# A 64-element pipeline on one core: key chunks in whole groups of four, the mask added in ScalarE's copy, one eps and one pow for two elements, and a PSUM bank moved from the scores to the expert layer

## The chip, the cores and the metric

The kernel runs on one core of a Trainium2 chip. A core has five engines with instruction streams of their own: TensorE (PE, matmuls), VectorE (DVE), ScalarE (ACT), GpSimd (POOL) and SyncE (SP, which issues the DMAs). They wait for each other by semaphores alone. The metric is the device time of one execution in microseconds (us); lower is better. 64 batch elements of 128 tokens by 128 channels pass through eight layers. The change touches the last two.

## What is computed

The reference, cut to those two layers (before each of them the input is normalised: mean subtracted, divided by the root of variance + 1e-5):

```python
# attention over 77 text keys, additive scores, one pair of gates per token
txt  = textual_features @ Ws;  feat = features @ W           # (64,77,128), (64,128,128)
h    = tanh(txt[:, None, :, :] + feat[:, :, None, :] + b)    # every token with every key
rho  = h @ w[:, 0]                                           # (64,128,77)
rho  = rho + (1 - q_masks)[:, None, :] * -1e30               # masked keys
att  = softmax(rho);  txt_h = att @ textual_features
x    = x + (tanh(txt_h @ Wcw.T + bcw) * features + tanh(txt_h @ Wcb.T + bcb))
# eight experts, each token to its best one, up to 1024 tokens for an expert over the whole batch
probs = softmax(xt @ wg);  mask = one_hot(argmax(probs), 8)
mask  = mask * (cumsum(mask, axis=0) - mask < 1024)
x     = x + gate * (mask * (xt @ W[e].T + b[e])) summed over e
```

## The kernel before, in words

`part_3` does these two layers, one batch element after the other. All steps of an element have names, `x3.*` for the attention, `r.*` for the score sums on TensorE, `t0`/`t1`/`t2` and `u0`/`u1` for the tanh of five key chunks, `f3.*` for the experts. Four tables (`PE_D`, `ACT_D`, `DVE_D`, `POOL_D`) set the order of the steps on each engine. One pass through a table is a *turn*; a step written `name@n` does, in turn p, its work for element p - n. So every engine works through the same list of steps 64 times, plus as many turns as the largest number behind an @, in which only some of the steps have an element. Each engine takes its list strictly in order: a step whose input is late holds up all that stands behind it on that engine. `Order.value(name, e)` is the semaphore value that says that this step of element e is done.

The way of element e before the change: VectorE takes mean and variance (`x3.stats`, `x3.aggr`, L2249, L2252); GpSimd adds eps (L2034), raises to the power -1/2 (L2037) and normalises (`x3.norm`, L2045); TensorE transposes (`x3.T`, L2160), ScalarE copies out of PSUM, TensorE projects text and features into bank `p_x` (`x3.proj`). For the 77 keys the sum text + feature is a 128-channel by 128-token tile for each key: VectorE makes keys 0 to 50 in three chunks of 17 (`x3.sum0` to `sum2`, tile `th`, L2268), GpSimd keys 51 to 76 in two chunks of 13 (`s.sum0`, `s.sum1`, tile `tl`, L2063). ScalarE takes the tanh in place (L2125, L2133). TensorE multiplies each key's tile with the vector w:

In `add`, key k goes to row a = k // 4 of group b = k % 4: the matmul writes the 32 partitions 32b to 32b+31 of the bank `p_rho`, by a weight tile of 32 columns of which one holds w (`tile_position=(0, 32 * b)`, so four keys with different b use different column quarters of the array). An f32 matmul is two instructions in the trace. The steps `r.rho0`, `r.rho1`, `r.rho2` take VectorE's chunks and `r.rhoP0`, `r.rhoP1` GpSimd's. Then ScalarE copies the bank out (`x3.rho`, tile `rs`, L2106), TensorE transposes it (`r.rhoT`, L2193) and adds the mask by a matmul of one row (L2194), VectorE takes the largest score (`x3.nmax`), ScalarE the exp, and so on to two gates per token, with which GpSimd ends the layer (`x3.y`, `x3.x`). There are two banks `p_rho`, for even and odd elements.

The expert layer normalises again (eps and pow of its own, L2034 and L2037), transposes (`f3.T`, L2211), routes (`f3.route`, L2214; `f3.nmax`, `f3.exp`, `f3.eq`, `f3.first`, `f3.pick`, L2303), counts places (`f3.place`, L2218, L2219), keeps those under the limit (`f3.keep`, `f3.kT`), multiplies by the experts (`f3.g`, L2228; `f3.xm`, L2311; `f3.y`, L2232 and L2234) and adds to x (`f3.out`, L2316). All its PSUM results but `p_g` lie in one bank `p_f`, so `f3.T` of element e waits for `f3.out` of e - 1. The mask is made in the part before, stored to `drop_rows` in memory and read back by SyncE as one row `drop`.

## Time and profile before

| what | value |
|---|---|
| median of 3 runs | 3001.69 us (2998.08 to 3005.58) |
| the profiled execution, its time | 3016.49 us |
| the profiled execution, its span | 3014.4 us |
| busy over the span: PE, DVE, ACT, POOL | 2681.1, 2458.3, 2251.8, 1419.1 us |
| the last part, from its first load issue to the end | 2193.6 to 3014.4 us |

The profile is one execution; its span runs from the first to the last instruction, and its time has 2.1 us more around the span. Times in the views are microseconds from the span's start. An engine's busy time is the union of its instructions; what is left is waiting. The last part fills the last 27% of the span.

### The profile page before, as it was taken

What the parts mean: (1) busy time and instruction counts of PE and PEld (TensorE: products, weight loads), DVE (VectorE), ACT (ScalarE), POOL (GpSimd) and SP (SyncE); (2) the same over time, 40 slices, a digit from 0 to 9 for tenths busy, and PEclk for the clock granted to TensorE, in tenths of its full rate; (3) what the DMA queues carried; (4) which work ended last, traced back from release to release, by engine and by line L of the source; (5) the groups of instructions that cost most, each with busy time, mean ns of one, the idle gap of its engine ahead of it and who ended that gap; (6) DMA issues with size and microseconds to landing.
All of it is one profiled execution on the core that took longest, in us unless ns stands there. A gap on an engine that the chain in (4) does not pass through costs nothing. (4 is left out here: it accounts for less than half of the span.)

```text
span 3014.4 us, 78117 instructions
## 1 busy us (share of the span) xinstructions
PE 2681.1 (89%) x28593; PEld 2003.6 (66%) x28593; DVE 2458.3 (82%) x6675; ACT 2251.8 (75%) x5270; POOL 1419.1 (47%) x2217
## 2 busy tenths in 40 slices
PE   6999999999999759979999998886669999999997
PEld 4666666666666549957767776332657777777776
DVE  5899989999999626559999997598668888888885
ACT  3899989999999614447777775298568888888884
POOL 1344434444444223335555552000068888888884
PEclk8999999999999869989999998899889999999998
DMA  1011111111111011101111110100210000000000
GB/s 50 27 35 52 56 38 35 35 35 35 35 34 31 20 55 49 48 21 34 34 34 34 34 33 16 27 0 0 77 38 16 16 16 18 16 16 16 17 15 8
DMA packets 177627, 91.14 MB, mean 30 GB/s; under 512 B 46339, under 2 KB 174021, under 8 KB 177251
## 3 DMA queue, kind: packets, MB, share of 16 engines
q1 hardware_dynamic: 171716, 76.85, 9.5%
q0 software_dynamic: 4096, 8.40, 0.9%
q8 instruction: 234, 3.83, 0.5%
q14 instruction: 141, 1.16, 0.1%
q10 hardware_dynamic: 1440, 0.90, 0.1%
HBM read 43.73 MB, written 42.36 MB: 29 GB/s over the span
## 5 line engine op out<-in xcount | busy, mean ns | idle before, releaser
L2268 DVE TENSOR_TENSOR th<-tf,p_x 128x2176 f32<-128x2176 f32 x192 | 463.2, 2413 | 8.0 <-ACT tf L2101 5.8
L2125 ACT ACTIVATE th<-th 128x2176 f32<-128x2176 f32 x192 | 386.4, 2012 | 0.0
L2063 POOL TENSOR_TENSOR tl<-tf 128x1664 f32<-128x1664 f32 x128 | 381.5, 2981 | 7.9 <-ACT tf L2101 7.9
L562 ACT ACTIVATE probf<-probf,colf 128x128 f32<-128x128 f32 x1024 | 313.2, 393 | 0.0
L2176 PE MATMUL p_rho<-th,late_w_row 128*32 128x128 f32 x6528 | 246.3, 276 | 0.0
L2176 PEld LDWEIGHTS p_rho<-th,late_w_row 128*32 128x32 f32 x6528 | 201.0, 110 | 15.2
L1675 PE MATMUL acc<-xnT_all,wT 128*128 128x512 f32 x384 | 181.8, 626 | 29.6 <-DVE tmax L1867 13.2
L2133 ACT ACTIVATE tl<-tl 128x1664 f32<-128x1664 f32 x128 | 202.8, 1585 | 3.6 <-POOL tl L2063 3.6
L452 POOL TENSOR_SCALAR col<-col 128x1 f32<-128x1 f32 x64 | 13.7, 214 | 395.5 <-DVE colc L887 344.5
L1094 POOL TENSOR_SCALAR col<-col 128x1 f32<-128x1 f32 x256 | 56.8, 222 | 271.5 <-DVE col L1383 191.6
L710 PE MATMUL fp<-ident,probf 128*128 128x128 f32 x1024 | 142.5, 284 | 24.6 <-ACT ygf L569 21.5
L566 ACT COPY probTf<-fp 128x1024 f32<-128x1024 f32 x128 | 129.5, 1012 | 46.3 <-PE fp L710 46.3
L1675 PEld LDWEIGHTS acc<-xnT_all,wT 128*128 128x128 f32 x384 | 73.5, 198 | 135.5 <-issue 83.5
L657 PE MATMUL xp<-ident,prob 128*77 128x128 f32 x1024 | 143.2, 284 | 20.0 <-DVE colc L903 18.8
L862 DVE TENSOR_TENSOR probf<-fs,causal 128x1024 f32<-128x1024 f32 x128 | 155.0, 1211 | 7.2 <-PE fs L698 7.2
L657 PEld LDWEIGHTS xp<-ident,prob 128*77 128x77 f32 x1024 | 115.0, 151 | 68.4 <-issue 65.8
L710 PEld LDWEIGHTS fp<-ident,probf 128*128 128x128 f32 x1024 | 114.7, 145 | 67.1 <-ACT ygf L569 48.5
L1097 POOL TENSOR_TENSOR col<-col,minus_half 128x1 f32<-128x1 f32 x256 | 146.3, 571 | 21.3
L698 PE MATMUL fs<-kblkf,qTf 32*128 32x512 f32 x512 | 149.5, 661 | 2.7 <-POOL kblkf L471 2.7
L865 DVE TENSOR_REDUCE colf<-probf 128x8 f32<-128x1024 f32 x128 | 149.1, 1203 | 0.0
L2027 POOL MEMSET cxT<- 128x51 f32 x9 | 0.8, 141 | 302.6 <-POOLq L1588 302.4
L1272 PE MATMUL p_gv<-w_conv,xqT 128*128 128x512 f32 x256 | 140.0, 629 | 0.0
(431 smaller groups left out, 8430.8 us busy)
## 6 DMA issues: line engine op xcount, KB each, us to landing
rows<-zeros SPq DMA_DIRECT2D x64, 256.0 KB, 2.4
cxT<-in_ctxT SPq DMA_DIRECT2D x128, 38.5 KB, 2.1
xb<-rows SPq DMA_DIRECT2D x67, 64.0 KB, 1.8
rows<-yb SPq DMA_DIRECT2D x67, 64.0 KB, 1.6
x<-in_x SPq DMA_DIRECT2D x64, 64.0 KB, 1.8
x_mid<-x SPq DMA_DIRECT2D x64, 64.0 KB, 1.5
z<-x_mid SPq DMA_DIRECT2D x64, 64.0 KB
x_next<-z SPq DMA_DIRECT2D x64, 64.0 KB, 1.5
```

The lines of the kernel that those rows point to most:

```text
L562: last = nc.scalar.activation(scores, scores, ACT.Exp, bias=colf[s][:, 16 + HALF * hf + h:17 + HALF * hf + h])
L657: last = nc.tensor.transpose(xp[0:KEYS, h // GROUP, (h % GROUP) * TOK:(h % GROUP + 1) * TOK], prob0[s][:, hf, h * KEYS:(h + 1) * KEYS], id ...
L698: last = nc.tensor.matmul(fs[:, b, :], qTf[s][g0:g0 + GROUP * HDIM, :], kblkf[s][g0:g0 + GROUP * HDIM, :, :], start=True, stop=True, tile_ ...
L710: last = nc.tensor.transpose(fp[:, h // GROUP, (h % GROUP) * TOK:(h % GROUP + 1) * TOK], probf[s][:, hf, h * TOK:(h + 1) * TOK], ident[:])
L862: nc.vector.tensor_tensor(scores, fs[:].rearrange("p b (h k) -> p (b h) k", h=GROUP), causal[:].unsqueeze(1).to_broadcast([128, HALF, TOK] ...
L865: nc.vector.tensor_reduce(colf[s][:, 16 + HALF * hf:16 + HALF * (hf + 1)], scores, X_AXIS, ALU.max, negate=True).then_inc(dve_done, DVE_L. ...
L1675: last = nc.tensor.matmul(acc[n][:, k, :], wT[:, m, k * CH:(k + 1) * CH], xnT_all[:, i * TTILE:(i + 1) * TTILE], start=True, stop=True)
L2063: nc.gpsimd.tensor_tensor(tl[i % NP][:, 0:shape[1], :], tf[s][:, POOLED[n]:POOLED[n + 1]].unsqueeze(2).to_broadcast(shape), tf[s][:, FEAT: ...
L2125: nc.scalar.activation(b, b, ACT.Tanh).then_inc(act_done, ACT_L.did(f"t{c}.tanh", e))
L2133: nc.scalar.activation(b, b, ACT.Tanh).then_inc(act_done, ACT_L.did(f"u{n}.tanh", e))
L2176: last = nc.tensor.matmul(p_rho[r][ROWS * b:ROWS * (b + 1), 0:TOK], w_row[:, ROWS - 1 - a:2 * ROWS - 1 - a], tanh[:, k, :], start=(a == 0) ...
L2268: nc.vector.tensor_tensor(th[i % NT][:, 0:shape[1], :], tf[s][:, CHUNK[n]:CHUNK[n + 1]].unsqueeze(2).to_broadcast(shape), p_x[r][:, AT:AT ...
```

## The change

Five things are changed in the last part. (1) VectorE's chunks are 16, 16 and 20 keys, GpSimd's 12 and 13. (2) The mask is no longer added by a matmul: `x3.rho` becomes an activation with the function Identity and a column `drop[:, e]` as its bias; that column tile is made once at the start by a transpose on TensorE and a copy on ScalarE, and the store to `drop_rows`, its load and their waits are gone. `r.rhoT` becomes one transpose instruction. (3) GpSimd's steps `x3.eps`, `x3.rstd`, `f3.eps`, `f3.rstd` become `n.eps` and `n.rstd`, each of which works on two columns, for `x3` of element j and `f3` of element j - 4; the means and variances lie in a new ring `mv`. (4) There is one bank `p_rho`; `r.rho0` of an element waits for `x3.rho` of the one before. The bank that comes free is `p_y` and takes `f3.place`, `f3.kT` and `f3.y`; `f3.T` waits only for `f3.pick` of the element before, and `f3.place` for its `f3.out`. Rings `xf`, `xfT`, `colf` have three buffers in place of two. (5) The four tables are new, and the largest number behind an @ is 9 in place of 6.

```diff
-    def __init__(self, text, count):
+    def __init__(self, text, count, longer=()):
+        longer = dict(longer)
         words = [(name, int(n or 0)) for name, _, n in (word.partition("@") for word in text.split())]
-        turns = range(count + max([n for _, n in words], default=0))
-        self.order = [(name, p - n) for p in turns for name, n in words if 0 <= p - n < count]
+        counts = {name: count + longer.get(name.partition(".")[0], 0) for name, _ in words}
+        turns = range(max([counts[name] + n for name, n in words], default=0))
+        self.order = [(name, p - n) for p in turns for name, n in words if 0 <= p - n < counts[name]]
...
 PE_D = """
-    f3.y@6 r.rho0@2 f3.T@5 r.rhoT@3 f3.route@5 r.rhoP0@2 r.rho1@2 f3.place@5 x3.T r.rhoP1@2 f3.kT@5 x3.proj f3.g@5
-    p.PT@3 r.rho2@2 p.gate@3
+    r.rho0@4 r.rhoT@5 r.rhoP0@4 f3.y@9 r.rho1@4 f3.T@7 f3.place@8 r.rhoP1@4 r.rho2@4 x3.T@2 p.PT@5 f3.kT@8
+    f3.route@7 x3.proj@2 p.gate@5 f3.g@8
 """
 ACT_D = """
-    x3.xT x3.exp@3 f3.kT@5 t0.tanh@1 x3.PT@3 x3.proj t1.tanh@1 u1.tanh@1 x3.gate@3 x3.rho@2 f3.xT@4 u0.tanh f3.exp@4
-    t2.tanh@1
+    t1.tanh@2 x3.gate@4 f3.exp@6 x3.proj@1 t2.tanh@2 x3.exp@3 u1.tanh@2 t0.tanh@1 f3.xT@5 u0.tanh@1 x3.xT x3.rho@2
+    x3.PT@3 f3.kT@6
 """
 DVE_D = """
-    f3.eq@6 f3.first@6 f3.pick@6 f3.stats@5 x3.nmax@4 f3.aggr@5 f3.keep@6 x3.sum1@2 x3.rden@4 f3.xm@6 x3.sum2@2
-    x3.gb@4 f3.out@6 x3.sum0@1 x3.stats f3.nmax@5 x3.aggr f3.rden@5
+    x3.sum0@3 f3.pick@8 x3.aggr@2 f3.out@9 f3.stats@6 x3.rden@5 f3.aggr@6 x3.sum1@3 f3.keep@8 x3.sum2@3 f3.nmax@7
+    x3.gb@5 f3.xm@8 f3.rden@7 x3.nmax@4 f3.eq@7 f3.first@7 x3.stats@1
 """
 POOL_D = """
-    f3.taken@5 x3.eps x3.rstd x3.norm f3.eps@4 s.sum1@1 f3.rstd@4 f3.norm@4 s.sum0 x3.y@3 x3.x@3
-"""
-
+    f3.norm@7 s.sum0@3 n.eps@2 n.rstd@2 x3.norm@2 f3.taken@7 s.sum1@3 x3.y@5 x3.x@5
+"""
+
+F3_LAG = 4
...
+    POOL_L = Order(POOL_D, BATCH, dict(n=F3_LAG))
+    NR, NX, NT, NF = 9, 4, 4, 3
     ROWS = 32
-    CHUNK = (0, 17, 34, 51)
+    CHUNK = (0, 16, 32, 52)
     CHUNKS = len(CHUNK) - 1
-    POOLED = (51, 64, KEYS)
+    POOLED = (52, 64, KEYS)
     POOLS = len(POOLED) - 1
     NP = 4
-    DTILE, PTILE = CHUNK[1], POOLED[1] - POOLED[0]
+    NV = F3_LAG + 2
+    DTILE = max(b - a for a, b in zip(CHUNK, CHUNK[1:]))
+    PTILE = max(b - a for a, b in zip(POOLED, POOLED[1:]))
...
-        drop = sb("drop3", [1, BATCH * WIDE], BF16)
+        before_bf, ones_bf, ident_bf, w_txt, w_feat, w_row, w_gate, b_gate, w_route, w_exp, pick_row, b_bf, drop_tile = (shared["late"][k] for k in (
+            "before_bf", "ones_bf", "ident_bf", "w_txt", "w_feat", "w_row", "w_gate", "b_gate", "w_route", "w_exp", "pick_row", "b_bf", "drop_tile"))
+        drop = sb("drop3", [128, BATCH])
...
-        p_rho = [ctx.enter_context(nc.psum_tensor(f"p_rho{s}", [128, BANK], F32)) for s in range(2)]
         p_x = [ctx.enter_context(nc.psum_tensor(f"p_x{s}", [128, BANK], F32)) for s in range(2)]
-        p_rT, p_f = (ctx.enter_context(nc.psum_tensor(n, [128, BANK], F32)) for n in ("p_rT", "p_f"))
+        p_rho, p_rT, p_f, p_y = (ctx.enter_context(nc.psum_tensor(n, [128, BANK], F32)) for n in ("p_rho", "p_rT", "p_f", "p_y"))
...
-            def rstd(p, e, c):
-                pool.wait_ge(dve_done, DVE_L.value(f"{p}.aggr", e))
-                nc.gpsimd.tensor_scalar(c[:, 8:9], c[:, 7:8], LN_EPS, None, ALU.add).then_inc(pool_done, POOL_L.did(f"{p}.eps", e))
-                yield
-                own(f"{p}.eps", e)
-                nc.gpsimd.tensor_tensor(c[:, 9:10], c[:, 8:9], minus_half[:, 0:1], ALU.pow).then_inc(pool_done, POOL_L.did(f"{p}.rstd", e))
+            def pair(j):
+                v = mv[j % NV]
+                here = slice(0 if j < BATCH else 1, 2 if j >= F3_LAG else 1)
+                n = here.stop - here.start
+                if j < BATCH:
+                    pool.wait_ge(dve_done, DVE_L.value("x3.aggr", j))
+                if j >= F3_LAG:
+                    pool.wait_ge(dve_done, DVE_L.value("f3.aggr", j - F3_LAG))
+                nc.gpsimd.tensor_scalar(v[:, 4 + here.start:4 + here.stop], v[:, 0:4].rearrange("p (n m) -> p m n", m=2)[:, 1, here], LN_EPS, None, ALU.add).then_inc(pool_done, POOL_L.did("n.eps", j))
+                yield
+                own("n.eps", j)
+                nc.gpsimd.tensor_tensor(v[:, 6 + here.start:6 + here.stop], v[:, 4 + here.start:4 + here.stop], minus_half[:, 0:n], ALU.pow).then_inc(pool_done, POOL_L.did("n.rstd", j))
                 yield
 
             def x3(e):
                 s, q = e % NX, e % NR
-                c = col[s]
-                yield from rstd("x3", e, c)
-                own("x3.rstd", e)
-                nc.gpsimd.tensor_scalar(xn[s][:], x[q][:], c[:, 6:7], c[:, 9:10], ALU.subtract, ALU.mult).then_inc(pool_done, POOL_L.did("x3.norm", e))
+                c, v = col[s], mv[e % NV]
+                own("n.rstd", e)
+                nc.gpsimd.tensor_scalar(xn[s][:], x[q][:], v[:, 0:1], v[:, 6:7], ALU.subtract, ALU.mult).then_inc(pool_done, POOL_L.did("x3.norm", e))
...
-                nc.scalar.copy(rs[r][:], p_rho[r][:, 0:TOK]).then_inc(act_done, ACT_L.did("x3.rho", e))
+                nc.scalar.activation(rs[r][:], p_rho[:, 0:TOK], ACT.Identity, bias=drop[:, e:e + 1]).then_inc(act_done, ACT_L.did("x3.rho", e))
...
+            act.wait_ge(drop_pe, 1)
+            nc.scalar.copy(drop[:], p_rT[:, 0:BATCH // 2].bitcast(BF16)).then_inc(drop_in, 1)
+            act.wait_ge(drop_in, 1)
...
-                    if c == 0 and e >= 2:
-                        pe.wait_ge(act_done, ACT_L.value("x3.rho", e - 2))
+                    if c == 0 and e >= 1:
+                        pe.wait_ge(act_done, ACT_L.value("x3.rho", e - 1))
...
-                nc.tensor.matmul(p_rT[:, 0:WIDE], rs[r][:], ident[:], start=True, stop=False)
-                nc.tensor.matmul(p_rT[:, 0:WIDE], ones_bf[0:1, :], drop[:, e * WIDE:(e + 1) * WIDE], start=False, stop=True).then_inc(pe_done, PE_L.did("r.rhoT", e))
+                nc.tensor.transpose(p_rT[:, 0:WIDE], rs[r][:], ident[:]).then_inc(pe_done, PE_L.did("r.rhoT", e))
...
                 if e >= 1:
-                    pe.wait_ge(dve_done, DVE_L.value("f3.out", e - 1))
-                nc.tensor.transpose(p_f[:, 0:TOK], xf[r][:], ident[:]).then_inc(pe_done, PE_L.did("f3.T", e))
+                    pe.wait_ge(dve_done, DVE_L.value("f3.pick", e - 1))
+                nc.tensor.transpose(p_f[:, 0:TOK], xf[s][:], ident[:]).then_inc(pe_done, PE_L.did("f3.T", e))
                 yield
                 pe.wait_ge(act_done, ACT_L.value("f3.xT", e))
-                nc.tensor.matmul(p_f[:, 128:128 + MOE3], xfT[r][:], w_route[:], start=True, stop=True).then_inc(pe_done, PE_L.did("f3.route", e))
+                nc.tensor.matmul(p_f[:, 128:128 + MOE3], xfT[s][:], w_route[:], start=True, stop=True).then_inc(pe_done, PE_L.did("f3.route", e))
                 yield
                 pe.wait_ge(pool_done, POOL_L.value("f3.taken", e))
                 pe.wait_ge(dve_done, DVE_L.value("f3.pick", e))
-                nc.tensor.matmul(p_f[:, 144:144 + MOE3], before_bf[:], pick[e % 4][:], start=True, stop=False)
-                nc.tensor.matmul(p_f[:, 144:144 + MOE3], ones_bf[:], taken[e % 4][:], start=False, stop=True).then_inc(pe_done, PE_L.did("f3.place", e))
+                if e >= 1:
+                    pe.wait_ge(dve_done, DVE_L.value("f3.out", e - 1))
+                nc.tensor.matmul(p_y[:, 144:144 + MOE3], before_bf[:], pick[e % 4][:], start=True, stop=False)
...
+            nc.tensor.transpose(p_rT[:, 0:BATCH // 2].bitcast(BF16), drop_tile[:], ident_bf[0:BATCH, 0:BATCH]).then_inc(drop_pe, 1)
+            pe.wait_ge(drop_in, 1)
```

How the tables put the instructions on the engines is best seen in the order itself. TensorE before, most of one turn in the steady state, from `f3.y` to the next `x3.T` and the second GpSimd chunk (the name of the tile written, the tiles read, its shape; xN is N keys or experts):

```order
L2232 MATMUL p_f<-late_b_bf,keptT 128x128
L2234 MATMUL p_f<-w_pair,xm 128x128 x8
L2176 MATMUL p_rho<-th,late_w_row 32x128 x17
L2211 MATMUL p_f<-ident,xf 128x128
L2193 MATMUL p_rT<-ident,rs 128x128
L2194 MATMUL p_rT<-drop,late_ones_bf 128x128
L2214 MATMUL p_f<-late_w_route,xfT 128x8
L2176 MATMUL p_rho<-tl,late_w_row 32x128 x13
L2176 MATMUL p_rho<-th,late_w_row 32x128 x17
L2218 MATMUL p_f<-pick,late_before_bf 128x8
L2219 MATMUL p_f<-taken,late_ones_bf 128x8
L2160 MATMUL p_x<-ident,xn 128x128
```

TensorE with the change, from the first score block of a turn to `x3.T`:

```order
L2186 MATMUL p_rho<-th,late_w_row 32x128 x16
L2203 MATMUL p_rT<-ident,rs 128x128
L2186 MATMUL p_rho<-tl,late_w_row 32x128 x12
L2243 MATMUL p_y<-late_b_bf,keptT 128x128
L2245 MATMUL p_y<-w_pair,xm 128x128 x8
L2186 MATMUL p_rho<-th,late_w_row 32x128 x16
L2220 MATMUL p_f<-ident,xf 128x128
L2229 MATMUL p_y<-pick,late_before_bf 128x8
L2230 MATMUL p_y<-taken,late_ones_bf 128x8
L2186 MATMUL p_rho<-tl,late_w_row 32x128 x13
L2186 MATMUL p_rho<-th,late_w_row 32x128 x20
L2170 MATMUL p_x<-ident,xn 128x128
```

The row of the mask (L2194) is gone. The blocks of a turn were 17, 13 + 17, 13 (behind `x3.T`) and 17 keys (later in the turn); now they are 16, 12, 16 and 13 + 20, where a + says that two chunks stand back to back. `f3.y` stood ahead of all of them and now stands between the second and the third, and `x3.T` follows the last of them at once.

VectorE before, from `f3.out` (L2316) on, where sum0 (L2268), the two moments of x3 (L2249, L2252) and the routing follow:

```order
L2316 SCALAR_TENSOR_TENSOR x<-p_f,colf,x 128x128
L2268 TENSOR_TENSOR th<-tf,p_x 128x2176
L2249 BN_STATS col<-x 128x6
L2290 TENSOR_REDUCE colf<-p_f 128x1
L2252 BN_AGGR col<-col 128x2
L2293 RECIPROCAL colf<-colf 128x1
```

VectorE with the change, the same neighbourhood:

```order
L2261 BN_STATS col<-x 128x6
L2282 TENSOR_TENSOR th<-tf,p_x 128x2048
L2319 TENSOR_SCALAR pick<-p_f,colf 128x8
L2264 BN_AGGR mv<-col 128x2
L2332 SCALAR_TENSOR_TENSOR x<-p_y,colf,x 128x128
L2261 BN_STATS colf<-x 128x6
L2289 RECIPROCAL col<-col 128x1
L2264 BN_AGGR mv<-colf 128x2
L2282 TENSOR_TENSOR th<-tf,p_x 128x2048
```

Before, the long sum stood between `f3.out`, which waits for `f3.y`, and the moments of x3; now the moments' first step stands ahead of sum0, `x3.aggr` (the first L2264) ahead of `f3.out`, and only two short rows between `f3.out` and `f3.aggr` (the second L2264).

GpSimd before, one turn from `x3.eps` on:

```order
L2034 TENSOR_SCALAR col<-col 128x1
L2037 TENSOR_TENSOR col<-col,minus_half 128x1
L2045 TENSOR_SCALAR xn<-x,col 128x128
L2034 TENSOR_SCALAR colf<-colf 128x1
L2063 TENSOR_TENSOR tl<-tf 128x1664
L2037 TENSOR_TENSOR colf<-colf,minus_half 128x1
L2074 TENSOR_SCALAR xf<-x,colf 128x128
L2063 TENSOR_TENSOR tl<-tf 128x1664
```

GpSimd with the change, from `n.eps` on:

```order
L2041 TENSOR_SCALAR mv<-mv 128x2
L2044 TENSOR_TENSOR mv<-mv,minus_half 128x2
L2051 TENSOR_SCALAR xn<-x,mv 128x128
L2089 TENSOR_TENSOR taken<-taken,pick 128x8
L2069 TENSOR_TENSOR tl<-tf 128x1664
L2055 TENSOR_SCALAR xn<-xn,col 128x128
L2058 TENSOR_TENSOR x<-xn,x 128x128
L2079 TENSOR_SCALAR xf<-x,mv 128x128
```

An eps and a pow of one column each are gone, and the remaining two work on two columns; the normalisation of the expert layer now stands most of a turn behind them.

## Rows read from the trace of the kernel before

**Rows 1.** Windows: us; busy of PE, PEld, DVE, ACT, POOL; PEclk; DMA share, GB/s.

```profile
2300.00:2900.00 600.00, 556.60 (x9845) 462.91 (x9843) 517.93 (x887) 528.14 (x793) 500.43 (x546) 1.00 0.06 17
2960.00:3014.40 54.40, 38.83 (x461) 31.90 (x453) 21.99 (x60) 17.34 (x40) 13.62 (x26) 0.81 0.03 8
```

**Rows 2.** Waits, 2300 to 2900 us: TensorE's; total us, times, longest.

```profile
PE p_x L2160 <- POOL xn L2045: 28.5, 49, 0.6
PE p_f L2218 <- DVE pick L2303: 14.0, 47, 0.3
```

**Rows 3.** Timeline of one turn: start, us, engine, line; in brackets the idle before.

```profile
2600.28 0.33 PE L2160 MATMUL p_x<-ident,xn 128*128 128x128 f32 x1 [0.58 <-POOL xn L2045]
2600.54 1.06 PE L2176 MATMUL p_rho<-tl,late_w_row 128*32 128x128 f32 x26
...
2603.51 1.28 PE L2176 MATMUL p_rho<-th,late_w_row 128*32 128x128 f32 x34
...
2605.19 2.05 PE L2234 MATMUL p_f<-w_pair,xm 128*128 128x128 f32 x16
...
2607.36 0.35 DVE L2316 SCALAR_TENSOR_TENSOR x<-p_f,colf,x 128x128 f32<-128x128 f32 x1 [0.32 <-PE p_f L2234]
...
2608.87 0.23 PE L2194 MATMUL p_rT<-drop,late_ones_bf 1*128 1x128 bf16 x1
...
2609.07 0.39 PE L2214 MATMUL p_f<-late_w_route,xfT 128*128 128x8 f32 x2
...
2610.56 0.23 POOL L2034 TENSOR_SCALAR col<-col 128x1 f32<-128x1 f32 x1 [1.58 <-DVE col L2252]
...
2611.54 0.81 POOL L2045 TENSOR_SCALAR xn<-x,col 128x128 f32<-128x128 f32 x1
...
2612.40 0.33 PE L2160 MATMUL p_x<-ident,xn 128*128 128x128 f32 x1 [0.58 <-POOL xn L2045]
```

**Rows 4.** Windows of L2176 alone, from the start of one block of 17 keys.

```profile
2615.63:2615.76 0.13, 0.13 (x4) 0.13 (x8) 1.00 0.00 0
2615.63:2616.50 0.87, 0.87 (x32) 0.87 (x33) 1.00 0.00 0
2615.63:2616.60 0.97, 0.97 (x33) 0.97 (x34) 1.00 0.00 0
2615.63:2616.70 1.07, 1.07 (x34) 1.01 (x34) 1.00 0.00 0
```

**Rows 5.** Groups by line and shape, whole span: busy us, mean ns, idle before.

```profile
L2268 DVE TENSOR_TENSOR th<-tf,p_x 128x2176 f32<-128x2176 f32 x192 | 463.2, 2413 | 8.0 <-ACT tf L2101 5.8 <-PE p_rho L2176 2.0
...
L2063 POOL TENSOR_TENSOR tl<-tf 128x1664 f32<-128x1664 f32 x128 | 381.5, 2981 | 7.9 <-ACT tf L2101 7.9
...
L455 POOL TENSOR_TENSOR colf<-colf,minus_half 128x2 f32<-128x2 f32 x64 | 46.4, 725 | 5.3
...
L2037 POOL TENSOR_TENSOR col<-col,minus_half 128x1 f32<-128x1 f32 x64 | 36.4, 568 | 5.3
...
L1143 ACT ACTIVATE qT<-p_gv,b_xa 128x128 f32<-128x128 f32 x64 | 23.5, 367 | 12.8 <-PE p_gv L1245 12.6
...
L2106 ACT COPY rs<-p_rho 128x128 f32<-128x128 f32 x64 | 15.3, 239 | 0.0
```

**Rows 6.** Timeline: the first sum, then `f3.out` and the last turn.

```profile
2202.09 2.42 DVE L2268 TENSOR_TENSOR th<-tf,p_x 128x2176 f32<-128x2176 f32 x1 [5.19 <-ACT tf L2101]
...
2255.66 0.35 DVE L2316 SCALAR_TENSOR_TENSOR x<-p_f,colf,x 128x128 f32<-128x128 f32 x1 [0.68 <-PE p_f L2234]
...
2970.10 0.35 DVE L2316 SCALAR_TENSOR_TENSOR x<-p_f,colf,x 128x128 f32<-128x128 f32 x1
...
3001.45 0.35 DVE L2316 SCALAR_TENSOR_TENSOR x<-p_f,colf,x 128x128 f32<-128x128 f32 x1 [4.17 <-PE p_f L2234]
...
3004.46 0.17 PE L2218 MATMUL p_f<-pick,late_before_bf 128*128 128x8 bf16 x1 [1.47 <-DVE pick L2303]
...
3012.05 0.35 DVE L2316 SCALAR_TENSOR_TENSOR x<-p_f,colf,x 128x128 f32<-128x128 f32 x1 [4.13 <-PE p_f L2234]
```

86 lines of the change are left out of this document (42 added, 44 removed).

## The prediction, made before the changed kernel ran

> **What bounds the kernel now.** I read the windows first, to see which stage the change touches and how full its engines are; then the waits of that stage, which name what an engine stood idle for; then the timeline of one turn, to follow the loop that sets its length. The reader is to see three things. In the steady state the granted clock is 1.00 (the 2.4 GHz level) and in 600 us PE is busy 556.6, ACT 528.1, DVE 517.9 and POOL 500.4 us [rows 1]: nobody is full. One turn lasts 2612.40 - 2600.28 = 12.12 us, from one `x3.T` to the next [rows 3]. So 600 us hold 49.5 turns, and one turn costs PE 11.24, ACT 10.67, DVE 10.46 and POOL 10.11 us of work. PE's missing 0.88 us are nearly two waits: for `x3.norm` (28.5 us in 49 turns, 0.58 each) and for `f3.pick` (0.3 each) [rows 2].
>
> The loop behind the first wait is in the timeline. PE goes from `x3.T` (2600.28) without a stop through its list to the end of `f3.y` (2605.19 + 2.05 = 2607.24); DVE has waited for this and makes `f3.out` at 2607.36; then its list has the long sum0 ahead of `x3.stats` and `x3.aggr`, so GpSimd starts eps only at 2610.56, after 1.58 us of idleness, and ends the normalisation at 2612.35; PE's next `x3.T` is at 2612.40 [rows 3]. That is 6.96 us of PE, 3.3 of DVE, 1.8 of POOL: the whole 12.12 us. PE alone would need 11.24. So two things are to be asked: what the new tables make of this loop, and what work each engine has per turn.
>
> **The change part by part.** *Key chunks.* Within a block of 17 keys (34 instructions) the starts come in bursts of four: 4 in the first 0.13 us, 32 by 0.87, and then the last two alone, one between 0.87 and 0.97 and one by 1.07 [rows 4]. So a burst step is about 0.11 us, four keys with their two instructions each take two steps, and the 17th key takes two more steps for itself. A check: the block of 13 keys has 6 full steps and 2 single ones, that is 7 intervals of 0.11 and one matmul of some 0.28, together 1.05; the row has 1.06 [rows 3]. The 17: 9 intervals, 1.00 + 0.28 = 1.28; the row has 1.28 [rows 3]. Counted in rounds of four keys, the blocks of a turn before are 17, 13 + 17, 13, 17: 5 + 8 + 4 + 5 = 22 rounds (in the double block the second chunk begins with the group that the first has just not used). Now they are 16, 12, 16 and 13 + 20. The last begins its second chunk with the same group that ended the first, so it takes 3 + 1 + 5 = 9, and the sum is 4 + 3 + 4 + 9 = 20. Two rounds less are 4 x 0.11 = 0.44 us of PE per turn. If there were nothing to the rounds and only the number of keys counted, it would be 0, since there are 77 before and after; both ends are kept.
>
> *The mask.* The matmul of one row began at 2608.87 and the next instruction at 2609.07: 0.20 us of PE per turn [rows 3]. The one-pass transpose may give 0.06 more; I take nothing. On ScalarE the copy of 239 ns becomes an Identity with a column as bias. The nearest row is L1143, the same function and shape out of PSUM with such a bias: 367 ns [rows 5], so ACT pays 0.13 us. The Trainium skill ("ScalarE: Activation LUTs", What ACT_TABLE_LOAD costs) puts a pointer operand at about 93 ns; by that the price would be 0.09, and 2 us less over 64 turns. The transpose and copy that make `drop` stand at the start of the part, where PE has nothing until the first x has come, and cost nothing; without that cover it would be under 1 us, once. The DMAs taken away from SP had no one waiting for them.
>
> *One key more for VectorE.* 2413 ns for 17 keys are 0.14 us a key [rows 5]: DVE +0.14. GpSimd's key is 2981 / 13 = 0.23 us less. ScalarE's tanh covers 77 keys as before.
>
> *eps and pow.* One eps of 0.23 [rows 3] and one pow of 0.57 go; the pow of two columns takes 0.725 (L455) in place of 0.568 [rows 5]. POOL: -0.23 - 0.57 + 0.16 - 0.23 = -0.87. It is no bound, so this is worth nothing by its size; what counts is where it stands.
>
> *The sums per turn.* PE 11.24 - 0.44 - 0.20 = 10.60; ACT 10.67 + 0.13 = 10.80; DVE 10.46 + 0.14 = 10.60; POOL 10.11 - 0.87 = 9.24. An engine's busy time is a little more than its need, since instructions whose inputs are there overlap, as `x3.T` and the block behind it by 0.07 [rows 3], so 10.6 is possible and 10.8 is what ACT's sum says. If the new tables let the engines run, a turn takes 10.8.
>
> *Do they?* The old loop is cut: `x3.stats` now stands ahead of sum0 and `x3.aggr` before `f3.out`, so no long sum lies between `f3.y` and the eps. What joins them now is the common eps, which also waits for `f3.aggr` of the element four behind. From the end of `f3.y`: 0.12 to `f3.out`, 0.3 for it, then `f3.stats`, the reciprocal and `f3.aggr`: 0.7 by estimate from the 0.23 of another short row, 1.05 if each took the 0.35 of `f3.out`; then 2.0 on POOL (2610.56 to 2612.35, and 0.16 for the wider pow) [rows 3, 5]. That is 3.1 to 3.4 us. In PE's list `r.rho1` (1.05), three short steps (0.2 each, as the mask's) and the double block (17 intervals of 0.11 and 0.28, 2.15) stand between `f3.y` and `x3.T`: 3.8, less 0.1 to 0.2 where they overlap. It arrives in time with 0.2 to 0.5 us to spare. I laid the other handovers out in this way, each engine's list from such durations; most have 0.1 to 0.5 us to spare at 10.6, `x3.rho` 2 us (below). With so many near the edge a few tenths of waiting would be no surprise: that is the range's upper part.
>
> *Filling and emptying.* Now: the first sum at 2202.09, `f3.out` of element 0 at 2255.66, of element 59 at 2970.10 (59 turns, 12.11 each), the end at 3014.4 [rows 1, 6]. With the change the largest lag is 9 in place of 6. Filling: 8.5 us to the first sum as now, then six turns up to the first `f3.out` instead of five. The five took (2255.7 - 2202.1) / 5 = 10.7 each, 1.4 less than a full one; six of 10.8 - 1.3 = 9.5 are 57, with the 2.5 us by which `f3.out` stands behind sum0 in DVE's list 68 in all, against 62. Then 57 full turns to `f3.out` of element 57: 57 x 10.8 = 616. Emptying: six turns, against four in 42 us. The two first still have most of the attention in them: 9.5 and 8. The last four hold the expert layer alone. Such a turn took 3012.05 - 3001.45 = 10.6, of which 2.7 lie between the end of `f3.out` and `f3.place`: transposing, routing and choosing [rows 6]. These no longer stand behind `f3.out`, since `f3.T` waits only for `f3.pick`: 8.0 each, 32. With the 2.3 us after the last `f3.out`: 52, against 44.
>
> **The sum.** The last part takes 68 + 616 + 52 = 736 us, against 3014.4 - 2193.6 = 820.8 now: -85. The profiled execution (span 3014.4, time 3016.5) becomes a span of 2930 and a time of 2932; it was 14.8 us above the median of the runs, so the median becomes 3001.7 - 85 = **2917 us** (-2.8%).
>
> **The rivals.**
> *Handovers bind* (0.20). The lists are right in their work, but one of the tight handovers costs each turn 0.3 to 0.9 us; the turn is 11.1 to 11.7. For it: three engines within 0.2 us of each other leave no room, and now they lose 1.3 to 1.6 us a turn. Against it: each loop that I followed closes below 10.6. At 11.4: 57 x 0.6 = +34, 2951 us.
> *Rounds don't count* (0.07). If a key costs the same in any block, PE keeps 11.04 and sets the turn: +14, 2931. The single last bursts speak against it [rows 4]. The Trainium skill ("TensorE: Matmul & The Clock Gate", Part 3: Packing small matmuls) has a group of column tiles take the time of one matmul plus some 4 ns each; the trace agrees with its bursts, and by that page an unfilled group costs a full one, as in my sum.
> *The single bank* (0.04), the one on the other side. With two banks PE could write one while ACT read the other; now `r.rho0` stops PE until ACT has read `p_rho`. Behind the last block PE has `x3.T`, four steps (2603.51 - 2600.28, less the block of 1.06: 2.2 with `x3.T`) and two pairs of 0.39: 2.9 us [rows 3]. The copy has to be done in that time, and in ACT's list a tanh of 12 keys and the copy after `x3.T` stand ahead of it; from `x3.T` on it needs 0.33 + 0.24 + 0.37 [rows 3, 5] and handovers, about 1.0. It decides when ACT runs 2 us behind; the gain is gone when each turn waits 1.5 us more than that. At 2 us of waiting a turn is 12.8: 68 + 730 + 52 = 850, 3031 us. The Trainium skill speaks for this rival ("PSUM — Partial Sum Buffer", Summary: rules for kernel authors: for reading PSUM while a matmul runs, target a different bank).
> *No change* (0.02): half of the two before, a turn of 12.2.
> *More than forecast* (0.07): the engines overlap better, a turn of 10.5, or the clock stays up in the emptying: 17 + 10 less, 2890.
>
> **How the numbers follow.** The forecast has 0.60, with a turn of 10.6 to 11.0, so 2905 to 2929 us. The range for 8 in 10 takes in the rounds, most of the handovers (up to 11.4 with a longer emptying) and part of the better case: 2896 to 2956. 0.3% (9 us) is about what a measurement of this kernel can tell from no change. Faster than that: 0.60 + 0.20 + 0.07 + 0.07 = 0.94, less 0.01 for handovers that add up to more; slower 0.04; the same 0.03.
>
> **What would show it.** Right: from the middle of the part on `x3.T` follows `x3.T` after 10.6 to 11.0 us; PE, ACT and DVE are each busy over 95%, POOL 85%; a block of 16 keys takes 1.05 to 1.1 us and the block of 13 + 20 about 2.15; L2111 takes 0.37 and L2044 on two columns 0.72; the last `f3.out` are 8 us apart. Wrong: a PE wait for `x3.rho` (the bank), for `x3.norm` above 0.1 us a turn (the common eps), blocks of 16 keys at 1.23 (the rounds), or a PEclk below 1.00 in the steady state, which no step above foresees.

## The result and the profile after

The changed kernel takes 2909.29 us (median of 4 runs, 2906.76 to 2914.39), the kernel before 3003.64 us beside it (4 runs, 2998.08 to 3007.85): a ratio of 0.9689, with a 95% interval of 0.9667 to 0.9711. That is 94.4 us or 3.1% less, where 85 less were forecast; the forecast of the time was 2917, range 2896 to 2956. (Of two kernels in the table below one execution each, 3314.24 us of b_chunks and 3401.13 us of a_old_tables, was in a slower state with a mean granted clock of 0.735 and 0.821; the medians hold them, the ratios don't.)

The profiled execution took 2907.73 us, with a span of 2905.9. Its first part of the page, the busy time of each engine with its share of the span:

```profile
PE 2624.1 (90%) x28466; PEld 1955.9 (67%) x28466; DVE 2450.1 (84%) x6675; ACT 2238.8 (77%) x5271; POOL 1369.0 (47%) x2097
```

The last part now begins at 2179.6 us and ends with the span: 726.3 us, against 820.8. The difference of 94.5 is that of the medians. (In this execution the last part also begins 14 us earlier than in the profile of before. The kernels run below, whose part ahead of it is the same as one or the other, begin it anywhere from 2177.1 to 2192.5 us, so these 14 us are spread between runs. I therefore compare lengths of the last part and of its turns. Each kernel has one profile, so how far these lengths are spread between executions is not known; within the profile of after, 52 of the 57 turns lie between 10.36 and 10.73 us.)

The windows of the steady state, to be laid beside [rows 1]:

```profile
2300.00:2800.00 500.00, 498.00 (x9341) 411.83 (x9339) 488.92 (x856) 496.16 (x761) 440.37 (x428) 0.99 0.07 19
```

PE is busy 99.6% of the time (before 92.8%), ACT 99.2% (88.0%), DVE 97.8% (86.3%), POOL 88.1% (83.4%). Three engines are full at once. The waits of the same stretch (total us, times, longest), beside [rows 2]:

```profile
POOL mv L2041 <- DVE mv L2264: 28.5, 47, 1.8
POOL xn L2055 <- ACT col L2123: 18.2, 47, 0.4
PEld p_x L2170 <- POOL xn L2051: 11.1, 47, 0.6
PEld p_rT L2203 <- ACT tf L2106: 9.1, 42, 0.4
```

PE's own waits for the normalisation (28.5 us before) and for `f3.pick` (14.0) are gone, but for 0.7 us in three turns. GpSimd, the lightest, waits 0.6 us a turn for the second aggregation. The PEld rows (weight loads, 0.2 us a turn each) are the first weight load behind a block of column tiles. The one of L2170 is put down to the normalisation, which in the turn below ends at 2602.58, only 0.06 ahead of `x3.T`; a_split below shows that it isn't what holds the turn. One turn of the timeline, from the VectorE row of one `f3.out` to that of the next, in which the rows of [rows 3] have their successors:

```profile
2599.56 0.32 DVE L2332 SCALAR_TENSOR_TENSOR x<-p_y,colf,x 128x128 f32<-128x128 f32 x1
...
2602.64 0.33 PE L2170 MATMUL p_x<-ident,xn 128*128 128x128 f32 x1
...
2603.16 0.39 PE L2223 MATMUL p_f<-late_w_route,xfT 128*128 128x8 f32 x2
2603.58 0.45 PE L2174 MATMUL p_x<-cxT,late_w_txt 128*128 128x77 f32 x2
...
2605.47 1.08 PE L2186 MATMUL p_rho<-th,late_w_row 128*32 128x128 f32 x32
2606.48 0.33 PE L2203 MATMUL p_rT<-ident,rs 128*128 128x128 f32 x1
2606.74 0.86 PE L2186 MATMUL p_rho<-tl,late_w_row 128*32 128x128 f32 x24
2607.53 0.23 PE L2243 MATMUL p_y<-late_b_bf,keptT 24*128 24x128 bf16 x1
...
2603.44 0.35 ACT L2111 ACTIVATE rs<-p_rho,drop 128x128 f32<-128x128 f32 x1
2603.70 0.24 ACT L2120 COPY probT<-p_rT 77x128 f32<-77x128 f32 x1
...
2609.98 0.32 DVE L2332 SCALAR_TENSOR_TENSOR x<-p_y,colf,x 128x128 f32<-128x128 f32 x1
```

The turn is 10.42 us. ScalarE ends its pass over the single bank at 2603.79, and `r.rho0` begins at 2605.47 with no wait: the bank has 1.7 us to spare. Two groups by line and shape over the whole span (busy, mean ns, idle before), beside [rows 5]:

```profile
L2044 POOL TENSOR_TENSOR mv<-mv,minus_half 128x2 f32<-128x2 f32 x60 | 43.2, 720 | 5.0
L2111 ACT ACTIVATE rs<-p_rho,drop 128x128 f32<-128x128 f32 x64 | 23.5, 366 | 2.4 <-PE p_rho L2186 2.4
```

VectorE's timeline at the two ends of the last part, beside [rows 6]: the first sum, the sum of the turn of the first `f3.out`, that `f3.out`, the one of element 57, and the last two.

```profile
2188.07 2.29 DVE L2282 TENSOR_TENSOR th<-tf,p_x 128x2048 f32<-128x2048 f32 x1 [4.85 <-ACT tf L2106]
...
2249.36 2.27 DVE L2282 TENSOR_TENSOR th<-tf,p_x 128x2048 f32<-128x2048 f32 x1
...
2252.84 0.35 DVE L2332 SCALAR_TENSOR_TENSOR x<-p_y,colf,x 128x128 f32<-128x128 f32 x1 [0.98 <-PE p_y L2245]
...
2853.87 0.35 DVE L2332 SCALAR_TENSOR_TENSOR x<-p_y,colf,x 128x128 f32<-128x128 f32 x1 [1.04 <-PE p_y L2245]
...
2895.64 0.35 DVE L2332 SCALAR_TENSOR_TENSOR x<-p_y,colf,x 128x128 f32<-128x128 f32 x1 [3.57 <-PE p_y L2245]
2903.60 0.35 DVE L2332 SCALAR_TENSOR_TENSOR x<-p_y,colf,x 128x128 f32<-128x128 f32 x1 [4.01 <-PE p_y L2245]
```

Filling took 2252.84 - 2179.58 = 73.3 us, 57 turns 601.0, emptying 52.0. But 57 x 10.42 is 593.9: 7.1 us more are there. Five of the 57 turns took 11.6 to 11.8 us (one of them from 2609.98 to 2621.74), together 6.5 us more than five of the others. Windows of 2 us through that one (PEclk is the third figure from the end):

```profile
2614.00:2616.00 2.00, 2.00 (x21) 1.69 (x25) 2.00 (x3) 2.00 (x4) 2.00 (x1) 1.00 0.04 8
2616.00:2618.00 2.00, 2.00 (x41) 1.38 (x43) 1.55 (x5) 2.00 (x6) 1.51 (x4) 0.62 0.00 0
2618.00:2620.00 2.00, 2.00 (x28) 1.45 (x21) 1.97 (x5) 2.00 (x4) 2.00 (x2) 0.53 0.00 0
2620.00:2622.00 2.00, 2.00 (x31) 1.88 (x33) 1.24 (x4) 2.00 (x2) 1.02 (x1) 1.00 0.00 0
```

The granted clock falls near its lower level (0.50, that is 1.2 GHz) for about 3.4 us (0.62 and 0.53 over 4 us) and comes back, though PE stood hardly idle before it (busy 1.97 and 2.00 of 2 us in the two windows from 2612). In [rows 1] the clock is 1.00.

### The profile page after: what moved, and what is told of

It reads as the page before. It is cut to its first block and busy times, and to the rows that moved or that the text cites. A ratio compares the mean times of both kernels' runs of the same rounds, so it can differ in the third digit from the quotient of the medians.

```text
span 2905.9 us, 77863 instructions
## 1 busy us (share of the span) xinstructions
PE 2624.1 (90%) x28466; PEld 1955.9 (67%) x28466; DVE 2450.1 (84%) x6675; ACT 2238.8 (77%) x5271; POOL 1369.0 (47%) x2097
## 5 line engine op out<-in xcount | busy, mean ns | idle before, releaser
L2282 DVE TENSOR_TENSOR th<-tf,p_x 128x2048 f32<-128x2048 f32 (+1 forms) x192 | 470.0, 2450 | 5.8 <-ACT tf L2106 5.5
L2130 ACT ACTIVATE th<-th 128x2048 f32<-128x2048 f32 (+1 forms) x192 | 393.1, 2047 | 2.5 <-DVE th L2282 2.4
L2069 POOL TENSOR_TENSOR tl<-tf 128x1536 f32<-128x1536 f32 (+1 forms) x128 | 368.4, 2878 | 5.9 <-ACT tf L2106 5.9
L2186 PE MATMUL p_rho<-th,late_w_row 128*32 128x128 f32 x6656 | 237.9, 279 | 0.0
L2138 ACT ACTIVATE tl<-tl 128x1536 f32<-128x1536 f32 (+1 forms) x128 | 196.1, 1532 | 0.0
L2186 PEld LDWEIGHTS p_rho<-th,late_w_row 128*32 128x32 f32 x6656 | 184.9, 110 | 14.0
L2245 PE MATMUL p_y<-w_pair,xm 128*128 128x128 f32 x1024 | 139.7, 293 | 0.0
```

Source lines behind the costliest of these rows:

```text
L2069: nc.gpsimd.tensor_tensor(tl[i % NP][:, 0:shape[1], :], tf[s][:, POOLED[n]:POOLED[n + 1]].unsqueeze(2).to_broadcast(shape), tf[s][:, FEAT: ...
L2130: nc.scalar.activation(b, b, ACT.Tanh).then_inc(act_done, ACT_L.did(f"t{c}.tanh", e))
L2138: nc.scalar.activation(b, b, ACT.Tanh).then_inc(act_done, ACT_L.did(f"u{n}.tanh", e))
L2186: last = nc.tensor.matmul(p_rho[ROWS * b:ROWS * (b + 1), 0:TOK], w_row[:, ROWS - 1 - a:2 * ROWS - 1 - a], tanh[:, k, :], start=(a == 0), s ...
L2245: last = nc.tensor.matmul(p_y[:, 256:256 + DIM], xm[r][:, n, :], w_exp[:, n, :], start=False, stop=(n == MOE3 - 1))
L2282: nc.vector.tensor_tensor(th[i % NT][:, 0:shape[1], :], tf[s][:, CHUNK[n]:CHUNK[n + 1]].unsqueeze(2).to_broadcast(shape), p_x[r][:, AT:AT ...
```

## The experiments

Each kernel's edit is against the changed kernel (names a_...) or the kernel before (b_...). The kernel before ran beside each group, at medians of 3006 to 3011 us. Medians of the kernel before move by up to 7 us between groups (3003.64 to 3010.65), so I read turn lengths (median spacing of `f3.out` over the first 57 turns of the profile) and the length of the last part as well.

| kernel | median us | ratio to before (95%) | turn us | long turns | last part us |
|---|---|---|---|---|---|
| before | 3003.64 | | 12.12 | 0 | 820.8 |
| after | 2909.29 | 0.9689 (0.9667, 0.9711) | 10.42 | 5 | 726.3 |
| a_old_chunks | 2921.35 | 0.9698 (0.9659, 0.9736) | 10.61 | 0 | 729.2 |
| a_no_mask | 2916.43 | 0.9686 (0.9652, 0.972) | 10.41 | 4 | 722.9 |
| a_mask_matmul | 2916.37 | 0.9689 (0.9657, 0.972) | 10.57 | 1 | 726.9 |
| a_split | 2907.62 | 0.9661 (0.9628, 0.9694) | 10.43 | 5 | 725.0 |
| a_merged | 2909.74 | 0.967 (0.9634, 0.9705) | 10.42 | 4 | 725.4 |
| a_lighter | 2903.52 | 0.9657 (0.9625, 0.9689) | 10.33 | 3 | 714.8 |
| a_merged_old_chunks | 2934.99 | 0.9761 (0.9746, 0.9777) | 10.72 | 13 | 750.1 |
| b_chunks | 3007.77 | 1.0003 (0.9984, 1.0022) | 12.00 | 1 | 816.9 |
| b_stats_first | 3101.0 | 1.0301 (1.0262, 1.0341) | 13.50 | 1 | 918.8 |
| b_stats_ring5 | 2968.73 | 0.9883 (0.9858, 0.9908) | 11.45 | 0 | 780.2 |
| a_old_all_tables | 3012.33 | 1.0023 (1.0006, 1.004) | 12.20 | 0 | 828.7 |
| a_old_tables | 3342.53 | 1.104 (1.0955, 1.1125) | 18.86 or 15.2 | - | 1167.8 |

A long turn is one more than 0.9 us above the median one. In a_old_tables turns of 18.9 and of 15.2 us mix, so the column means little there; they average 18.05 over 57 turns.

### What each light edit is worth in the new order

**The old chunks.**

```diff
-    CHUNK = (0, 16, 32, 52)
+    CHUNK = (0, 17, 34, 51)
-    POOLED = (52, 64, KEYS)
+    POOLED = (51, 64, KEYS)
```

> The changed kernel (turn 10.42 us, 2909 us) with the key chunks of before: 17, 17, 17 for VectorE, 13 and 13 for GpSimd; all else as changed. Blocks on TensorE are then 17, 13, 17 and 13 + 17 keys, 5 + 4 + 5 + 8 = 22 rounds of four in place of 20. Theory A (rounds count, and TensorE is full at 10.42): the turn grows by 4 burst steps of 0.11 = 0.44 us to 10.86, and 61 turns of that make +27 us, 2936 us. Theory B (only the number of keys counts): 10.4, 2909 us; VectorE even loses 0.13 us of work per turn. Theory C (ScalarE alone sets the turn, and TensorE has 0.2 us to spare): 10.65, 2924 us.

The turn is 10.606 us. PE's timeline in a_old_chunks, where the block of 17 keys fills 1.21 us to the next row (16 keys: 1.01) and the one of 13 fills 1.00 (12 keys: 0.79):

```profile
2605.95 1.28 PE L2186 MATMUL p_rho<-th,late_w_row 128*32 128x128 f32 x34
2607.16 0.33 PE L2203 MATMUL p_rT<-ident,rs 128*128 128x128 f32 x1
2607.41 1.06 PE L2186 MATMUL p_rho<-tl,late_w_row 128*32 128x128 f32 x26
2608.41 0.23 PE L2243 MATMUL p_y<-late_b_bf,keptT 24*128 24x128 bf16 x1
```

Over the turn the five chunks cost PE 0.4 us more (three times 0.2, less 0.21 for the last pair). So rounds of four keys count, as the step said, and half of the 0.4 is seen, since the other half is room that PE has: in after, `x3.proj` begins 0.18 us later behind `f3.route` (2603.16, 2603.58) than in a_old_chunks (2603.84, 2604.08), because it waits for ScalarE's copy, which ends at 2603.53.

**The mask left out**, so ScalarE's pass is the plain copy; the output differs where keys are masked.

```diff
-                nc.scalar.activation(rs[r][:], p_rho[:, 0:TOK], ACT.Identity, bias=drop[:, e:e + 1])
+                nc.scalar.copy(rs[r][:], p_rho[:, 0:TOK])
```

> The changed kernel with a plain copy in place of the Identity with a bias, so the mask is left out of the scores (the output is another one for masked keys). ScalarE has 0.12 us less work per turn, all else is the same. Theory A (ScalarE, which shows no idle in the changed kernel, is the engine that sets the turn): 10.42 becomes 10.30, -8 us, 2901 us. Theory B (TensorE is as full and holds the turn): 10.42 stays, 2909 us.

ScalarE's timeline of a_no_mask; the next row now begins 0.16 us behind the start of the copy, and 0.26 behind that of the Identity in after:

```profile
2570.21 0.30 ACT L2111 COPY rs<-p_rho 128x128 f32<-128x128 f32 x1
2570.37 0.28 ACT L2120 COPY probT<-p_rT 77x128 f32<-77x128 f32 x1
```

So the bias costs 0.10 us of ScalarE, but the median turn becomes only 0.01 shorter (10.41): ScalarE alone does not hold the turn.

**The mask by the matmul again** (with its store, its load and the plain copy).

```diff
-                nc.tensor.transpose(p_rT[:, 0:WIDE], rs[r][:], ident[:])
+                nc.tensor.matmul(p_rT[:, 0:WIDE], rs[r][:], ident[:], start=True, stop=False)
+                nc.tensor.matmul(p_rT[:, 0:WIDE], ones_bf[0:1, :], drop[:, e * WIDE:(e + 1) * WIDE], start=False, stop=True)
```

> The changed kernel with the mask added by a one-row matmul again, as before: ScalarE 0.12 us less per turn, TensorE 0.20 to 0.26 us more. Theory A (TensorE is full): turn 10.62 to 10.68, +12 to +16 us, 2921 to 2925 us. Theory B (ScalarE alone sets the turn and TensorE has room): 10.30, 2901 us. In between: the difference from 10.42 + 0.23 is what TensorE had to spare.

PE's timeline of a_mask_matmul:

```profile
2606.71 0.49 PE L2205 MATMUL p_rT<-ident,rs 128*128 128x128 f32 x2
2607.13 0.23 PE L2206 MATMUL p_rT<-drop,late_ones_bf 1*128 1x128 bf16 x1
2607.28 0.86 PE L2188 MATMUL p_rho<-tl,late_w_row 128*32 128x128 f32 x24
```

0.57 us in place of 0.26: 0.31 more on PE, of which 0.15 reach the turn (10.57). The rest, 0.16, is again room that PE had. The last part is only 0.6 us longer: the 57 turns take 3.6 us more (each is 0.15 longer, and there are four long turns fewer), and the filling takes 3.7 us less.

**eps and pow apart.**

```diff
-    f3.norm@7 s.sum0@3 n.eps@2 n.rstd@2 x3.norm@2 f3.taken@7 s.sum1@3 x3.y@5 x3.x@5
+    f3.norm@7 s.sum0@3 x3.eps@2 x3.rstd@2 x3.norm@2 f3.eps@6 f3.rstd@6 f3.taken@7 s.sum1@3 x3.y@5 x3.x@5
```

> The changed kernel with an eps and a pow for each of the two normalisations again (x3.eps, x3.rstd ahead of x3.norm; f3.eps, f3.rstd behind it), so GpSimd has 0.23 + 0.57 - 0.16 = 0.64 us more per turn. Theory A (GpSimd is no bound: it waits 0.6 us for f3.aggr and 0.4 us for the gate in each turn now): turn 10.4 to 10.45, within 3 us of 2909. It can be a little faster, since x3.norm no longer waits for f3.aggr (TensorE's x3.T waits 0.2 us for it now): then 10.3, 2903 us. Theory B (the pair is needed, GpSimd's later sums hold ScalarE up): the turn grows by 0.2 to 0.6 us, 2921 to 2946 us.

The turn is 10.43 and the last part 725.0 us, as in after (726.3): the pair is worth nothing here. GpSimd is busy 468.7 of 500 us instead of 440.4 and still waits. Here `x3.norm` no longer waits for `f3.aggr`, yet the weight load of `x3.T` still stands 0.2 us (9.1 us in 46 turns, now put down to nobody), so in after too the common eps is not what holds the turn.

### What holds 10.42

**One block fewer on PE.**

```diff
-    r.rho0@4 r.rhoT@5 r.rhoP0@4 f3.y@9 ...
+    r.rho0@4 r.rhoP0@4 r.rhoT@5 f3.y@9 ...
-    ... t2.tanh@2 x3.exp@3 u1.tanh@2 t0.tanh@1 ...
+    ... t2.tanh@2 u1.tanh@2 x3.exp@3 t0.tanh@1 ...
-    x3.sum0@3 f3.pick@8 x3.aggr@2 ... f3.rden@7 x3.nmax@4 f3.eq@7 ...
+    x3.sum0@3 x3.nmax@5 f3.pick@8 x3.aggr@2 ... f3.rden@7 f3.eq@7 ...
```

> The changed kernel with r.rhoP0 set directly behind r.rho0 on PE, so that the two make one block of column tiles of 28 keys, and x3.nmax and u1.tanh moved with it. In the trace of after PE stands 0.2 us behind each such block before the next matmul; one block less gives PE 0.2 us a turn. My theory: in the changed kernel three engines are within 0.2 us of one another (ScalarE's list without a gap is 10.42, VectorE's 10.37, PE's own about 10.25), so more room on PE gives nothing: the turn stays 10.42. Rival: PE is what holds 10.42 and the turn is 10.2 to 10.3, 7 to 12 us less. A loss would show that the moved nmax or the tanh is now late.

The turn stays 10.42. The two blocks with `r.rhoT` take 1.93 us in place of 2.06, and PE's busy time in 500 us falls from 498.0 to 494.2: PE is lighter and the turn is the same.

**The same with ScalarE and VectorE lighter too**: the mask is left out, and the two moments' first steps and the maximum are taken over half of their columns (so the output is another one).

```diff
-                nc.vector.bn_stats(c[:, 0:6], x[s][:])
+                nc.vector.bn_stats(c[:, 0:6], x[s][:, 0:DIM // 2])
-                nc.vector.tensor_reduce(c[:, 16:17], p_rT[:, 0:WIDE], X_AXIS, ALU.max, negate=True)
+                nc.vector.tensor_reduce(c[:, 16:17], p_rT[:, 0:WIDE // 2], X_AXIS, ALU.max, negate=True)
```

> The kernel a_merged with less work on the two other engines: ScalarE's pass over p_rho is the plain copy (the mask is left out), and VectorE's x3.stats, f3.stats and x3.nmax take half of their columns, some 0.2 us less a turn; so statistics and maximum are over half of the data. Taking ScalarE's 0.1 alone gave 10.405, PE's 0.2 alone gave 10.42. Theory: the three lists are equal within 0.1 to 0.2 us (ScalarE 10.36 without the mask, VectorE 10.37), so only the three together show: turn 10.30 to 10.36, ScalarE without a gap, 3 to 6 us less in the last part. Rival: something else holds 10.4 (a loop of handovers) and the turn stays at 10.40.

The turn is 10.33 and the last part 11.5 us shorter than after's (3 to 6 expected; the 57 turns take 8.2 us less, with three long turns, not five, and the filling and the emptying, which have the lighter work too, 2.8 and 0.6 less). So 10.42 is not held by one handover that the lighter work leaves as it is, but by lists of nearly one length. Taking 0.1 us from ScalarE's alone gives 0.01 us and taking 0.13 from PE's alone nothing; taking 0.1 to 0.2 from all three gives 0.09. VectorE alone, and any two of the three, were not made lighter, so which list comes next behind ScalarE's is not shown; by the runs above PE has 0.16 to 0.2 to spare.

**The old chunks in a_merged.**

> The changed kernel with the old key chunks (17, 17, 17 and 13, 13) and the merged block of a_merged. In the profiles so far turns of 11.7 us, with the granted clock near its lower level for some 3 us, come every ten to twelve turns in the kernels with turns of 10.32 to 10.55 us that have the new chunks (five in after, four to five in a_split and a_merged, one in a_mask_matmul), and none in a_old_chunks. Here PE has 0.2 us less than in a_old_chunks, 10.606 - 0.2 = 10.41, with ScalarE's 10.42 beside it. Theory: the dips belong to the blocks of the new chunks; the turn is 10.42 to 10.45 without dips and the last part some 5 us shorter than after's, time about 2905. Rival: they come with any turn near 10.4, whatever the blocks, then the time is that of after or a little more, 2909 to 2915.

Both fell. The turn is 10.72, longer than in either parent, and 13 of 57 turns are long. ScalarE's timeline of a_merged_old_chunks shows what is late:

```profile
2276.29 1.58 ACT L2138 ACTIVATE tl<-tl 128x1664 f32<-128x1664 f32 x1
2278.05 0.33 ACT L2116 ACTIVATE prob<-p_rT,col 128x80 f32<-128x80 f32 x1 [0.18 <-DVE col L2286]
```

The moved `x3.nmax` now stands behind a sum of 17 keys and comes 0.18 us late for the exp, in nearly every turn (8.3 us, 45 times in 500 us): a handover binds, the mechanism that the prediction had as a rival and that the changed kernel does not have. And the long turns are not bound to the new chunks.

### What cuts the old loop

**The new chunks alone in the kernel before** (`CHUNK` and `POOLED` as in the change).

> The kernel before with the new key chunks alone (16, 16, 20 and 12, 13). My theory: the turn of before is a loop from one x3.T to the next, and of PE's work in it only what stands between x3.T and f3.y counts; its blocks with fewer rounds there are the second pooled or the first, plus a sum0 that is one key shorter (0.14 us). Block P0 of 13 keys becomes 12 (-0.11 to -0.22), rho1 becomes 16 (-0.22) and neither r.rho2 (behind f3.y) counts. So the turn is 11.6 to 11.9 instead of 12.12, by the part that lies in the loop, and the time is 15 to 30 us less. Rival, the sum0 alone: 11.98, 8 us less. If PE's whole work counted in addition to the waits, the turn would lose 0.44 and the time 26 us.

The turn is 12.00, 0.12 less: the shorter sum0 alone, the rival. My own theory was wrong because I credited blocks that lie outside the loop; between `x3.T` and `f3.y` stand a block of 13 keys (13 after) and one of 17 (20 after, five rounds as well). The total shows no difference. One turn of 16.2 us, with a granted clock of 0.50 from 2712 to 2720 us behind two PE waits of 0.73 and 0.63 us, costs 4.2; in the last part (816.9) it takes back more than half of what the shorter turns give.

**The moments ahead of `f3.out` in the kernel before.**

```diff
-    x3.gb@4 f3.out@6 x3.sum0@1 x3.stats f3.nmax@5 x3.aggr f3.rden@5
+    x3.gb@4 x3.stats x3.aggr f3.out@6 x3.sum0@1 f3.nmax@5 f3.rden@5
```

> The kernel before with one edit of order: on VectorE x3.stats and x3.aggr stand ahead of f3.out and the long sum0 instead of behind them. It does the one thing that I named as what cuts the old loop, with the old work. My theory: the 0.58 us of waiting before x3.T go, and f3.nmax, behind sum0, comes 0.2 us earlier for f3.pick; the turn is 11.3 to 11.5 instead of 12.12, and the time about 44 us less (2955 to 2965). Rival: another loop of near the same length (by f3.nmax, f3.exp and f3.pick, which PE's f3.place awaits) keeps the turn above 11.9 and the gain is under 12 us.

Slower by 3%, with a turn of 13.5: neither theory. VectorE's timeline of b_stats_first:

```profile
2614.21 0.21 DVE L2279 SCALAR_TENSOR_TENSOR col<-p_rT,col,late_b_gate 128x2 f32<-128x2 f32 x1
2616.63 0.29 DVE L2249 BATCH_NORM_STATS2 col<-x 128x6 f32<-128x128 f32 x1 [2.21 <-POOL x L2052]
2616.96 0.18 DVE L2252 BATCH_NORM_AGGREGATE col<-col 128x2 f32<-128x6 f32 x1
2617.05 0.34 DVE L2316 SCALAR_TENSOR_TENSOR x<-p_f,colf,x 128x128 f32<-128x128 f32 x1
```

`x3.stats` writes a column of the ring `col3`, four deep, and so waits for GpSimd's `x3.x` of the element four before, the last long thing in GpSimd's turn. Moved ahead, it holds `f3.out` up with it. A loop through GpSimd takes the place of the old one: x3.x, the moments, f3.out, sum0 and the routing up to `f3.aggr`, GpSimd's f3.eps and the rest of its list.

**The same with that ring (and its sisters) five deep.**

```diff
-    NR, NX, NT = 9, 4, 4
+    NR, NX, NT = 9, 5, 4
```

> The kernel before with x3.stats and x3.aggr moved ahead of f3.out, as in b_stats_first, and with the rings of the attention part (the column col3 that x3.stats writes, among others) five deep instead of four. In the profile of b_stats_first VectorE waits 2.21 us a turn, at x3.stats, for GpSimd's x3.x of the element four before, with f3.out queued behind it, and PE's f3.T waits 1.7 us for f3.out. Theory: that wait is the ring's, and with one buffer more the old loop is really cut. What is left is f3.y, 0.12 us, f3.out, sum0 and the chain up to f3.pick (3.65), 0.4 to f3.place, 0.1 to x3.T, then 6.9 of PE: 11.2 to 11.4 us a turn, 12.12 before, so 40 to 50 us less than before. Rival: the wait for f3.out at f3.T (both use one PSUM bank) or the wait of the eps for f3.aggr keeps the turn above 12, and only the bank and the lags of the changed kernel can take it away.

The wait is gone, and the rows in VectorE's timeline of b_stats_ring5 stand close:

```profile
2600.62 0.21 DVE L2279 SCALAR_TENSOR_TENSOR col<-p_rT,col,late_b_gate 128x2 f32<-128x2 f32 x1
2600.75 0.29 DVE L2249 BATCH_NORM_STATS2 col<-x 128x6 f32<-128x128 f32 x1
2601.07 0.18 DVE L2252 BATCH_NORM_AGGREGATE col<-col 128x2 f32<-128x6 f32 x1
2601.17 0.34 DVE L2316 SCALAR_TENSOR_TENSOR x<-p_f,colf,x 128x128 f32<-128x128 f32 x1
```

The turn is 11.45 (11.2 to 11.4 expected) and the last part 40.6 us shorter. Of the change's 94.5 us, cutting this one edge of the loop, with the buffer that it needs, gives 41 by itself, without a lighter engine, a bank of its own for the expert layer or new lags. Where the other 54 come from was not taken apart further: the new chunks are worth 0.19 us a turn in the new orders and the mask in ScalarE's pass 0.15, and the new orders with the old banks or the old lags were not run.

**The changed code with all four old orders** (and eps and pow apart).

> The changed kernel's code (key chunks, mask in ScalarE's pass, single bank for scores and a bank of its own for the expert layer, rings of three) with separate eps and pow and with all four orders of before. Theory: this is the share of the change that is not the orders. The loop of before stays, of which only sum0 is 0.14 shorter; r.rho0 waits some 0.7 us for x3.rho in the single bank, but that lies where PE waits for x3.norm anyway; the lighter PE does not count. Turn 11.98 to 12.05, time 2992 to 3000 us, within 0.3% of before. Rivals: the single bank shows (turn 12.3 or more, slower than before), or the lighter work counts (11.6 or less, 30 us faster). With a_old_tables beside it, which differs from this kernel only in the pair, the difference is the pair's in the old order.

The turn is 12.20 us. PE's timeline of a_old_all_tables:

```profile
2569.38 1.08 PE L2182 MATMUL p_rho<-th,late_w_row 128*32 128x128 f32 x32 [0.81 <-ACT rs L2107]
```

The single bank does make PE wait in the old order, 0.81 us a turn. It takes the place of the wait for `x3.norm` (0.6 us a turn in b_chunks, none here), and a little more: the turn is 12.20 where b_chunks has 12.00 (that these 0.20 are the bank's alone is not shown, since the kernels differ in the mask and the rings too). By the Trainium skill ("PSUM — Partial Sum Buffer", Summary: rules for kernel authors) one reads PSUM during a matmul from another bank; this run shows a price of doing otherwise, 0.81 us of waiting, and after shows that an order with 1.7 us between the two pays none. So in the old orders all that the change does apart from them gives nothing (+0.2%), the bank's price included.

**The pair in the old order.** This kernel differs from the last one only in the pair.

```diff
-    f3.norm@7 s.sum0@3 n.eps@2 n.rstd@2 x3.norm@2 f3.taken@7 s.sum1@3 x3.y@5 x3.x@5
+    f3.taken@5 n.eps n.rstd x3.norm s.sum1@1 f3.norm@4 s.sum0 x3.y@3 x3.x@3
```

> The changed kernel with all its code edits (key chunks, mask, pair, single bank, rings) but with the orders of PE, ScalarE and VectorE of before, and on GpSimd the order of before with the pair in place of the two single eps and pow. My theory: the gain is the new orders', and the old ones do not fit the pair. GpSimd starts eps at 2610.56 in the profile of before, right after x3.aggr; the pair also waits for f3.aggr, which stands six steps later on VectorE and ends at 2611.95, so the loop grows by 1.4 us, by 0.16 for the wider pow, less 0.14 for a sum0 of 16 keys: turn 13.5 us against 12.12, 58 turns, some +80 us: about 3085 us. Rival: the lighter engines matter more than the order, and the turn is 12.1 or less, 3000 us or below. Second rival: the single bank adds a wait of its own to that.

Slower by 10%. A turn of 15.16 us (2575.43 to 2590.59) of the timeline of a_old_tables, GpSimd and PE, and PE's clock in windows of 2 us:

```profile
2579.68 0.17 DVE L2264 BATCH_NORM_AGGREGATE mv<-colf 128x2 f32<-128x6 f32 x1
...
2580.02 0.23 POOL L2041 TENSOR_SCALAR mv<-mv 128x2 f32<-128x2 f32 x1 [6.26 <-DVE kept L2323]
...
2582.01 0.33 PE L2170 MATMUL p_x<-ident,xn 128*128 128x128 f32 x1 [2.34 <-POOL xn L2051]
...
2582.27 1.91 PE L2186 MATMUL p_rho<-tl,late_w_row 128*32 128x128 f32 x26
```

```profile
2580.00:2582.00 2.00, 0.00 (x0) 0.00 (x0) 2.00 (x1) 0.87 (x1) 1.79 (x4) 1.00 0.00 0
2582.00:2584.00 2.00, 1.99 (x28) 1.62 (x28) 0.34 (x2) 0.59 (x3) 2.00 (x1) 0.56 0.03 8
2584.00:2586.00 2.00, 2.00 (x11) 1.43 (x10) 0.00 (x0) 1.67 (x2) 1.68 (x2) 0.59 0.00 0
```

The eps starts when `f3.aggr` (the row of 2579.68; the bracket names the row right behind it) is done, 1.6 us behind `x3.aggr` (2578.22 to 2578.40). Then PE stands idle for 2.34 us and works on at the lower level of its clock: the block of 13 keys takes 1.91 us, 1.06 at the upper one. In the turns of 18.9 us the clock is low for about three times as long (10 us, 0.50 from 2600 to 2608). From the start of `x3.T` to that of L2177 PE takes 3.58 us here and 2.18 in a_old_all_tables at full clock, so the low stretch costs about 1.4 us. That leaves 13.8 of the 15.16, where I had forecast 13.5 for the pair. The clock makes 18.05 of it on average. Whether the order could hold a steady 13.8 at full clock was not tried.

## Why the prediction was right, and where its terms were off

- **The loop.** The step "the old loop is cut" held, and the orders are what cuts it: cutting one edge in the old kernel gives 11.45 us a turn, the new orders 10.42, and the changed code in the old orders takes 12.20. What I had not seen is that the edge alone can't be cut: VectorE's moments also hang on a ring four deep, and without one more buffer the move costs 3%. In the new orders `x3.stats` stands one turn behind, at the end of VectorE's list, and does not wait.
- **Rounds of four keys.** Right in size: 0.4 us of PE by the blocks in both timelines, 0.44 forecast; the block of 13 + 20 takes 2.15 (2600.55 to 2602.70), as forecast. Worth 0.19 of a turn, since PE has 0.2 to spare.
- **The mask.** PE was forecast 0.20 lighter and is 0.31, because the transpose in one pass is shorter too, which I took as nothing; 0.15 of it reach the turn. ScalarE's Identity takes 366 ns against 239, as forecast from L1143, but its place in a full list grows by only 0.10: what counts there is the distance of the starts. The Trainium skill ("ScalarE: Activation LUTs", What ACT_TABLE_LOAD costs) has 93 ns for the pointer operand and an overlap of some 93 ns between ACTIVATEs back to back; both agree with the rows, by starts (0.10 for the column, 0.09 of overlap behind the Identity of 2603.44).
- **The turn, 10.8 forecast and 10.42 measured: the mis-sized term.** I took an engine's busy time per turn of before as its need (ACT 10.67 + 0.13). But an instruction ahead of an idle stretch counts to its very end, while in a full list the next one starts about 0.1 us before that (the copy of 2603.70 in after begins 0.09 before the Identity has ended). ScalarE stood idle in three places of a turn before, two of which its timeline in the kernel before shows:

```profile
2601.03 0.20 ACT L2111 ACTIVATION_READ_ACCUMULATOR prob<-p_rT,col 128x1 f32 x1
2601.70 0.25 ACT L2147 COPY keptT<-p_f 24x128 bf16<-24x128 bf16 x1 [0.46 <-PE p_f L2222]
...
2607.64 0.24 ACT L2106 COPY rs<-p_rho 128x128 f32<-128x128 f32 x1
2608.75 0.27 ACT L2141 COPY xfT<-p_f 128x128 f32<-128x128 f32 x1 [0.88 <-PE p_f L2211]
```

(The third, of 0.1 us, is ahead of L2094.) Where such rows stand without a gap, the next starts 0.09 behind the first and 0.14 behind the second, not 0.20 and 0.24; the three together make about 0.3 of the 0.38 by which 10.80 was too much. The rest is in starts that lie a little closer in after, and no run varied any of this alone. I had noted the overlap and then went by the sum all the same. Per turn 0.38 us, over 57 turns 22 us too much.
- **The clock**, which no step foresaw (0.99 in the steady state, one of my signs of being wrong), gave back 7.1 us of these: 616 forecast, 601.0 measured for the 57 turns.
- **Filling**: 73.3 us, 68 forecast; what makes it longer stays open. The first sum came after 8.5 us as said; the six turns took 2249.36 - 2188.07 = 61.3 us, 10.2 each where I had 9.5, and `f3.out` stood 3.5 us behind sum0, 2.5 forecast. **Emptying**: 52.0, as forecast; the last `f3.out` are 7.6 to 8.3 apart. In sum -15 and +5 against the forecast: 726.3 for 736.
- **Luck.** The time of 2909 lies within the 2905 to 2929 that I had tied to a turn of 10.6 to 11.0 us, and the turn does not lie there. The clock (+7) and the filling (+5), neither of which I saw, took back 12 of the 22 us by which the turn was too long. The mechanism held; that the number is as near as it is, is in part luck.
- **The rivals.** The single bank has 1.7 us to spare (2 forecast), and its price is real in another order. Handovers do not bind in the changed kernel, though the common eps is tighter than I had it (0.06 us to spare for 0.2 to 0.5); a_merged_old_chunks shows how little it takes. "More than forecast" was in part what happened: its better overlap came, its emptying did not.

## What to carry to other kernels

When several engines are near full, find the loop in the timeline first and count work only inside it; the new chunks were worth 0.12 us a turn in the old order, by a shorter sum on VectorE alone, and 0.19 in the new one, and the merged eps and pow nothing in the new order and, in the old one, 3 us a turn at the least, the wrong way, with what the clock lost by it. Before you move a step forward on an in-order engine, list everything it waits for, ring buffers too, and what stands behind it. And size an engine's need by the distances between starts in a stretch where it has no gap, not by its busy time in a stretch with gaps.

## What the runs showed of the hardware

- TensorE's granted clock fell near its lower level for about 3.4 us at a time in kernels where PE is busy over 98% (498.0 of 500 us in after, with five long turns; 492.9 in a_merged_old_chunks, with 13), and not in a_old_chunks (499.3 of 500) or b_stats_ring5 (486.9). Each time costs a turn 1.2 to 1.5 us. What sets it off stays open: it is not the blocks of the new chunks alone, and it does not go with the busy share.
- An idle stretch of PE of 2.3 us was followed by the lower level in a_old_tables, in the turns of 15.2 us it cost about 1.4 us, and in those of 18.9 about 5, by an estimate of 13.8 us for a turn at full clock, from the rows above.
- A group of four column tiles that is not filled costs a whole round: 17 keys fill 1.21 us and 16 fill 1.01; 13 fill 1.00 and 12 fill 0.79. Behind each block of column tiles the next weight load stood 0.2 us (the PEld rows); one block fewer gave PE 0.13 us.
